# Sixteen-head attentions: the first sequence's key rows sent from SyncE's queue behind the queries' rows instead of from ScalarE's

## The chip, the cores and the metric

The kernel runs on one core of one Trainium2 chip. The metric is the device time of one execution in microseconds. A core has TensorE (PE; its weight loads are listed as PEld), VectorE (DVE), ScalarE (ACT), GpSimd (POOL) and SyncE (SP), each with its own stream of instructions, and 16 DMA engines. A DMA is issued by one of the engines' queues (here SyncE's, ScalarE's or GpSimd's), occupies that engine while it is issued, and adds to a semaphore when its data has landed.

## What is computed

Four decoder layers, each of three blocks (attn, xattn, ffn), on 8 sequences of 256 tokens with 128 features; every block is added to x. Three of the twelve blocks concern the change. All are attentions of sixteen heads with eight features a head:

```python
# L1_xattn: queries and keys from normalised x, values from the context, causal, then a two-layer GELU block
q = (kq @ Wq + bq); k = (kq @ Wk + bk); v = (ctx @ Wv + bv)        # each as [8, 16 heads, 256, 8]
out = softmax(q k^T + shifted causal mask) v
y = gelu(out @ W1 + b1) @ W2 + b2
# L2_xattn: queries from normalised x, keys and values from the context, a drawn mask, scale 128 ** -0.5
out = softmax(where(mask == 0, -1e20, q k^T) / sqrt(128)) v;  y = out @ Wo.T + bo
# L3_attn: latent attention of x, causal, scale 8 ** -0.5
```

## The kernel before

One function, `attention16` (line 983), does all three: x1 (L1_xattn, tiles named x_), x2 (L2_xattn, tiles named x_ too) and a3 (L3_attn, tiles named a_). The eight sequences are eight units; the sixteen heads of a unit are taken in eight pairs. Scores have to be near to float32, but the matmuls run in bf16: so queries and keys are each split in three bf16 pieces (GpSimd, `split_in_three`, L1130 to L1133), and the six products of pieces that matter (`PRODUCTS`) are stacked along the contraction. A stack has eight rows for each of the eight features of a head: six rows of pieces, one row for the maxima and one of zeros. The rows are laid into `queries` and `keys` by DMA from `pieces`, one DMA for each of the six rows on each side.

SyncE does that, in `stack(u)` for unit u: it waits until the queries' pieces are made (`split`), sends one row of zeros (L1088) and six rows of queries, waits for the keys' pieces and sends six rows of keys (L1092). These thirteen DMAs count on `stacked[u % 2]`. Unit 0 is an exception in the kernel before: SyncE leaves its keys out (`continue`), and ScalarE sends them in `stack_first_keys` (L1484), after its copy of unit 0's values. `set_constant_rows(ring)` (L1071, L1073) sends three rows that don't depend on data, once for each of four rings: for ring 0 at the very start, for rings 1 to 3 behind unit 0's stack. In x2 SyncE also loads the mask twice for each unit (L1079). `store_rows(u)` (L1097) sends the maxima's pieces into the queries.

The work runs by slots, one slot for each pair, each engine with the same list of slots. Ahead of the scores, unit u is normalised (VectorE L1158), turned (TensorE L1275, copied by ScalarE to `xnT`, L1447), projected to queries (L1281, ScalarE L1453), keys (L1285, L1453) and values (L1292, L1462). Units 0 and 1 go through this before the first scores. TensorE's order at the start is thus: tokens, queries, keys, values of unit 0; the same of unit 1; the scores of pairs 0 to 7 (L1310, masks L1330 or L1334), with unit 2's projections between; the scores of pair 8, the first of unit 1; the turning of unit 0's maxima (L1355). The scores of pair 0 wait for `stacked[0]`, those of pair 8 for `stacked[1]`:

```python
                if p == 0:
                    pe.wait_ge(stacked[u % 2], (u // 2 + 1) * STACK_DMAS * 16)
```

VectorE takes the maxima of each pair (L1170, L1171, L1173) and after eight pairs splits them in pieces (L1184 to L1188); the shifted scores, TensorE's L1322 from slot 12 on, wait for the stored rows of maxima, and ScalarE's exponentials (L1469) for them. GpSimd may make the next unit's pieces only when the last unit's thirteen DMAs have landed:

```python
                if u >= 1:
                    pool.wait_ge(stacked[(u - 1) % 2], ((u - 1) // 2 + 1) * STACK_DMAS * 16)
```

Of the kernel before, what the change touches and what calls it, by code (L numbers as in the profile page):

```python
# [982 lines left out]
def attention16(nc, g, w, name, tag, scale, from_x, causal, values_from_x=False, tail=None):  # L983
# [3 lines left out]
    PRODUCTS = ((0, 0), (1, 0), (2, 0), (0, 1), (1, 1), (0, 2))  # L987
    STEP = 8
# [14 lines left out]
    with ExitStack() as ctx:  # L1003
# [5 lines left out]
        pieces = sb("pieces", [P, 2, PIECES, T], BF16)  # L1009
        queries, keys = (sb(n, [P, RINGS, PAIRS, T], BF16) for n in ("queries", "keys"))  # L1010
# [10 lines left out]
        else:  # L1021
# [9 lines left out]
        xn_ready, xT_made, q_made, k_made, v_made, split = (  # L1031
            sem(n) for n in ("xn_ready", "xT_made", "q_made", "k_made", "v_made", "split"))
        tokens_taken, q_taken, k_taken, v_taken, maxima_taken, mix_taken, y_taken = (
            sem(n) for n in ("tokens_taken", "q_taken", "k_taken", "v_taken", "maxima_taken", "mix_taken", "y_taken"))
        stacked, rows_stored = ([sem(f"{n}{b}") for b in range(2)] for n in ("stacked", "rows_stored"))
# [11 lines left out]
        norm_in, tokens_in, q_in, k_in, v_in = (lambda slot, early=e: unit_at(slot + early) for e in (13, 12, 11, 10, 9))  # L1047
# [20 lines left out]
        @block.sync  # L1068
        def _(sp):
            def set_constant_rows(ring):  # L1070
                sp.dma_start(keys[MAX_ROW::STEP, ring, :, :], max_keys[:, :]).then_inc(constant_rows[ring], 16)  # L1071
                for dst in (queries, keys):
                    sp.dma_start(dst[MAX_ROW + 1::STEP, ring, :, :], zeros[:, :]).then_inc(constant_rows[ring], 16)  # L1073

            def load_masks(u):
                if u >= 2:
                    sp.wait_ge(mask_ready, u - 1)
                for i, which in enumerate((g.mask_qk, g.mask_kq)):
                    sp.dma_start(mask_int[:, u % 2, i, :, :], which[u * HALVES:(u + 1) * HALVES, :, :].rearrange("n p k -> p n k"))\  # L1079
                      .then_inc(mask_loaded[u % 2], 16)  # L1080

            def stack(u):
                for which, dst in enumerate((queries, keys)):
                    sp.wait_ge(split, 2 * u + which + 1)
                    if which == 0:
                        if u >= RINGS:
                            sp.wait_ge(shifted, (u - RINGS + 1) * PAIRS)
                        sp.dma_start(queries[MAX_ROW::STEP, u % RINGS, :, :], zeros[:, :]).then_inc(stacked[u % 2], 16)  # L1088
                    if which == 1 and u == 0:
                        continue  # L1090
                    for slot, of in enumerate(PRODUCTS):
                        sp.dma_start(dst[slot::STEP, u % RINGS, :, :], pieces[:, which, of[which], :]).then_inc(stacked[u % 2], 16)  # L1092

            def store_rows(u):
                sp.wait_ge(max_split, u + 1)
                for k in range(PIECES):
                    sp.dma_start(queries[MAX_ROW + STEP * k::STACK, u % RINGS, :, :], max_pieces[:, u % 2, k, :])\  # L1097
                      .then_inc(rows_stored[u % 2], 16)

            sp.wait_ge(max_keys_ready, 2)  # L1100
            set_constant_rows(0)
            for slot in slots:
                if norm_in(slot) is not None and not causal:
                    load_masks(norm_in(slot))
                if maxima_in(slot) is not None:
                    store_rows(maxima_in(slot))
                if v_in(slot - 1) is not None:
                    stack(v_in(slot - 1))
                if v_in(slot - 1) == 0:
                    for ring in range(1, RINGS):  # L1110
                        set_constant_rows(ring)
# [327 lines left out]
        @block.scalar  # L1439
        def _(a):  # L1440
            a.wait_ge(g.loaded[name], 16)

            def take_tokens(u):
                a.wait_ge(xT_made, u + 1)
                if u >= 1:
                    a.wait_ge(v_made, u)
                a.activation(xnT[:, :], ps_p[:, 0:T], ACT.Copy).then_inc(tokens_taken, 1)  # L1447

            def take_projection(which, u):
                a.wait_ge((q_made, k_made)[which], u + 1)  # L1450
                if u >= 1:
                    a.wait_ge(split, 2 * u)
                a.activation(rest[:, which, :], ps_p[:, 0:T], ACT.Identity, bias=w[("q_bias", "k_bias")[which]])\  # L1453
                    .then_inc((q_taken, k_taken)[which], 1)

            def take_values(u):
                a.wait_ge(v_made, u + 1)
                if u == 0:
                    a.wait_ge(ones_ready, 1)
                if u >= KEPT:  # L1460
                    a.wait_ge(weighed, (u - KEPT + 1) * GROUPS)
                a.activation(v_ones[:, u % KEPT, :, :, 0:HD].rearrange("p j h d -> p (j h) d"),  # L1462
                             ps_p[:, 0:T].rearrange("p (n d) -> p n d", d=HD), ACT.Copy).then_inc(v_taken, 1)

            def take_probs(r):
                a.wait_ge(shifted, r + 1)
                if r >= HELD:
                    a.wait_ge(weighed, (r - HELD) // 2 + 1)
                a.activation(probs[:, r % HELD, :, :], ps_z[:, :, 0:WIDE], ACT.Exp, scale=scale).then_inc(exped, 1)  # L1469

            def take_sums(n):
                a.wait_ge(weighed, n + 1)
                if n >= 2:
                    a.wait_ge(back_made, n - 1)
                a.activation(sumsT[:, n % 2, :], ps_o[:, 0:T], ACT.Copy).then_inc(sums_ready, 1)

            def take_mixed(u):
                a.wait_ge(mixT_made, u + 1)
                a.activation(mixT[:, u, :], ps_p[:, 0:T], ACT.Copy).then_inc(mix_taken, 1)

            def stack_first_keys():
                a.wait_ge(split, 2)
                for slot, of in enumerate(PRODUCTS):
                    a.dma_start(keys[slot::STEP, 0, :, :], pieces[:, 1, of[1], :]).then_inc(stacked[0], 16)  # L1484

            for slot in slots:
                r = slot - BEHIND
                if sums_in(r) is not None:
                    take_sums(sums_in(r))
                if pair_at(r) is not None:  # L1490
                    take_probs(r)
                if tail and mix_in(r) is not None:
                    take_mixed(mix_in(r))
                if tokens_in(slot) is not None:
                    take_tokens(tokens_in(slot))
                if q_in(slot) is not None:
                    take_projection(0, q_in(slot))
                if k_in(slot) is not None:
                    take_projection(1, k_in(slot))
                if v_in(slot) is not None:  # L1500
                    take_values(v_in(slot))
                if v_in(slot) == 0:
                    stack_first_keys()
            if tail == "mlp":
                for t in range(TURNS):
                    for c in range(4):
                        a.wait_ge(up_made, t * 4 + c + 1)
                        if t >= 2:
                            a.wait_ge(mlp_made, t - 1)
                        a.activation(hT[:, t % 2, c, :], ps_s[:, c // 2, c % 2, :], ACT.Gelu, bias=w["b1"][:, c:c + 1])\  # L1510
                            .then_inc(gelu_ready, 1)
# [2159 lines left out]
```

## Time and profile before

| what | value |
|---|---|
| median of 3 runs | 2074.45 us (2067.26 to 2081.59) |
| profiled execution, span | 2099.1 us (the page gives no time around the span) |
| TensorE matmul busy | 1629.8 us (78%) |
| VectorE busy | 1224.3 us (58%) |
| ScalarE busy | 846.3 us (40%) |
| GpSimd busy | 456.8 us (22%) |
| mean granted TensorE clock | 0.840 |
| x1 begins | at about 364 us |
| x2 begins | at about 997 us |
| a3 begins (after its weights are combined) | at about 1398 us |

Issuing a DMA isn't counted as busy; it stands in an engine's timeline as SPq or ACTq. A row of the timeline gives start, duration (of a merged group from the first start to the last end), engine, line, operation, output and inputs, the number of instructions, and in brackets the idle time before it with what ended it.

### The profile page before, as it was taken

What the parts mean: (1) busy time and instruction counts of PE and PEld (TensorE: products, weight loads), DVE (VectorE), ACT (ScalarE), POOL (GpSimd) and SP (SyncE); (2) the same over time, 40 slices, a digit from 0 to 9 for tenths busy, and PEclk for the clock granted to TensorE, in tenths of its full rate; (3) what the DMA queues carried; (4) which work ended last, traced back from release to release, by engine and by line L of the source; (5) the groups of instructions that cost most, each with busy time, mean ns of one, the idle gap of its engine ahead of it and who ended that gap; (6) DMA issues with size and microseconds to landing.
All of it is one profiled execution on the core that took longest, in us unless ns stands there. A gap on an engine that the chain in (4) does not pass through costs nothing. (4 is left out here: it accounts for less than half of the span.)

```text
span 2099.1 us, 34839 instructions
## 1 busy us (share of the span) xinstructions
PE 1629.8 (78%) x12344; PEld 1130.1 (54%) x12368; DVE 1224.3 (58%) x4316; ACT 846.3 (40%) x1790; POOL 456.8 (22%) x611
## 2 busy tenths in 40 slices
PE   3359556798957887757699889968867777999888
PEld 2138343455525776755254456744535654677666
DVE  5965745476176898844566333337747776666322
ACT  1133326255323776753255434324543310333322
POOL 0002000320013334320532000012202114655111
PEclk8665777699978898978799989978987866999979
DMA  2000000321015567640522000012210000000000
GB/s 82 0 11 1 9 29 19 89 52 36 1 66 190 196 211 254 216 165 7 153 66 61 2 17 0 0 56 59 57 67 1 0 0 1 3 2 2 3 0 21
DMA packets 79748, 115.69 MB, mean 55 GB/s; under 512 B 8416, under 2 KB 60512, under 8 KB 78816
## 3 DMA queue, kind: packets, MB, share of 16 engines
q0 software_dynamic: 18432, 67.38, 9.3%
q1 hardware_dynamic: 58560, 45.00, 7.7%
q8 instruction: 96, 1.57, 0.3%
q10 hardware_dynamic: 2592, 1.18, 0.2%
q14 instruction: 68, 0.56, 0.1%
HBM read 88.95 MB, written 1.05 MB: 43 GB/s over the span
## 5 line engine op out<-in xcount | busy, mean ns | idle before, releaser
L2398 POOL DMA_INDIRECT f_rows<-tree_table,f_index x128 | 125.8, 983 | 312.9 <-DVE f_index L2458 153.5
L1469 ACT ACTIVATE x_probs<-x_ps_z 128x768 f32<-128x768 f32 (+1 forms) x128 | 117.4, 917 | 101.9 <-PE x_ps_z L1334 66.0
L2615 PE MATMUL f_ps_o<-f_rows,shared_sb 128*128 128x128 f32 x1024 | 127.8, 287 | 33.6 <-ACT f_rows L2687 33.6
L2687 ACT ACTIVATE f_rows<-f_rows,f_low_act 128x128 f32<-128x128 f32 x512 | 153.0, 387 | 0.8
L2615 PEld LDWEIGHTS f_ps_o<-f_rows,shared_sb 128*128 128x128 f32 x1024 | 123.2, 201 | 39.0 <-ACT f_rows L2687 34.9
L2497 DVE CUSTOM_DVE_ANT_0 f_rows<-f_rows,f_xn 128x128 f32<-128x128 f32 x512 | 112.6, 287 | 20.7 <-DMA f_rows<-tree_table,f_index 13.2
L1173 DVE TENSOR_REDUCE x_minus_max<-x_ps_s 128x4 f32<-128x1024 f32 x64 | 78.1, 1224 | 61.8 <-PE x_ps_s L1334 61.5
L3133 ACT ACTIVATE r_probs<-r_ps_z 128x768 f32<-128x768 f32 x64 | 51.9, 811 | 67.8 <-PE r_ps_z L3024 67.8
L1867 PE MATMUL f_ps_h<-f_xnT,weights 128*128 128x512 f32 x144 | 76.2, 657 | 2.4 <-ACT f_hT L1932 2.4
L1879 PEld LDWEIGHTS f_ps_y<-weights,f_hT 128*128 128x128 f32 x576 | 69.8, 192 | 14.3 <-issue 12.6
L1932 ACT ACTIVATE f_hT<-f_ps_h,weights 128x512 f32<-128x512 f32 x72 | 48.6, 685 | 71.6 <-PE f_ps_h L1867 69.9
L1846 DVE SCALAR_TENSOR_TENSOR x_tokens<-f_ps_y,f_chosen,x_tokens 128x128 f32 (+1 forms) x128 | 36.0, 344 | 68.1 <-PE f_ps_y L1879 67.9
L1879 PE MATMUL f_ps_y<-weights,f_hT 128*128 128x128 f32 x576 | 73.3, 278 | 0.0
L1469 ACT ACTIVATE a_probs<-a_ps_z 128x768 f32<-128x768 f32 x64 | 51.9, 810 | 41.7 <-PE a_ps_z L1330 41.6
L1347 PE MATMUL x_ps_o<-x_probs,x_v_ones 128*32 128x256 f32 (+1 forms) x1024 | 64.9, 361 | 2.5 <-DVE x_mixed L1198 2.5
L2597 PE MATMUL f_ps_in<-shared_sb,f_act 128*128 128x128 f32 x192 | 34.5, 350 | 39.5 <-ACT f_maskedT L2674 26.0
L1322 PE MATMUL x_ps_z<-x_queries,x_keys 64*128 64x256 bf16 (+1 forms) x512 | 47.5, 264 | 20.7 <-ACT x_probs L1469 18.0
L3015 PE MATMUL r_ps_z<-r_queries,r_keys 64*128 64x256 f32 (+1 forms) x512 | 59.1, 349 | 2.6 <-ACT r_probs L3133 2.5
L2605 PE MATMUL f_ps_d<-weights,f_maskedT 128*128 128x128 f32 (+2 forms) x384 | 56.9, 302 | 5.0 <-ACT f_maskedT L2674 5.0
L2889 DVE TENSOR_REDUCE r_minus_max<-r_ps_s 128x2 f32<-128x256 f32 x64 | 27.2, 425 | 56.9 <-PE r_ps_s L3024 56.9
L1170 DVE TENSOR_REDUCE x_minus_max<-x_ps_s 128x2 f32<-128x256 f32 x64 | 27.0, 422 | 54.0 <-PE x_ps_s L1330 53.7
L2833 POOL TENSOR_TENSOR r_q_swapped<-r_q_swapped,weights 128x256 f32<-128x256 f32 x64 | 46.5, 726 | 54.2 <-DVE r_q_swapped L2881 53.9
(652 smaller groups left out, 4145.2 us busy)
## 6 DMA issues: line engine op xcount, KB each, us to landing
x_queries<-x_pieces SPq DMA_DIRECT2D x96, 64.0 KB, 2.1
x_keys<-x_pieces SPq DMA_DIRECT2D x84, 64.0 KB, 2.1
a_queries<-a_pieces SPq DMA_DIRECT2D x48, 64.0 KB, 2.1
weights<-w_L_ffn SPq DMA_DIRECT2D x1, 2985.5 KB, 10.2
a_keys<-a_pieces SPq DMA_DIRECT2D x42, 64.0 KB, 2.1
weights<-w_L_ffn SPq DMA_DIRECT2D x1, 2449.0 KB, 10.5
weights<-w_L_ffn SPq DMA_DIRECT2D x1, 2176.0 KB, 8.3
f_rows<-tree_table,f_index POOLq DMA_INDIRECT x128
```

The source lines that it names most:

```text
L1173: last = v.tensor_reduce(peaks.rearrange("p j h -> p h j"), scores.rearrange("p h (j k) -> p h j k", j=HALVES), AX.X, ALU.max, negate=True)
L1347: last = pe.matmul(out[V1 * i:V1 * (i + 1), a:T], v_ones[:, u % KEPT, half, SIDE * group + i, :], probs[:, r % HELD, i % 2, at:at + T - a] ...
L1469: a.activation(probs[:, r % HELD, :, :], ps_z[:, :, 0:WIDE], ACT.Exp, scale=scale).then_inc(exped, 1)
L1867: pe.matmul(ps_h[:, i % 2, :], w["up"][:, i * P:(i + 1) * P], xnT[:, :], start=True, stop=True).then_inc(up_made, 1)
L1879: last = pe.matmul(out, hT[:, i % 4, j * P:(j + 1) * P], w["down"][:, i * P:(i + 1) * P], start=c == 0, stop=c == CH - 1 and e < E)
L2398: pool.indirect_dma_start(rows[:, place(u, j), tree, :], None, g.tree_table, bass.IndirectOffsetOnAxis(index[:, u % 2, low, j * TREES + tr ...
L2497: last = v.tensor_tensor_reduce(row, row, xn[:, u % KEPT, j, :], 1.0, 0.0, ALU.mult, ALU.add, low_act[:, u % 3, j * TREES + tree, f:f + 1])
L2605: last = pe.matmul(ps_d[:, j, :], maskedT[0:k, i, :], w["out"][0:k, i * P:(i + 1) * P], start=i == 0, stop=i == ALL - 1)
L2615: last = pe.matmul(ps_o[:, low, j, :], g.ident, rows[:, place(u, j), tree, OUT + f * D:OUT + (f + 1) * D], start=k == 0, stop=k == TREES * ...
L2687: last = a.activation(row, row, ACT.Copy, scale=low_act[:, u % 3, j * TREES + tree, f:f + 1])
L3015: pe.matmul(ps_z[:, i, out], keys[rows, u % RINGS, k:k + P], queries[rows, u % RINGS, p, q:T], start=q == 0, stop=False)
L3133: a.activation(probs[:, r % HELD, :, :], ps_z[:, :, 0:WIDE], ACT.Exp).then_inc(exped, 1)
```

## The change

SyncE no longer leaves out unit 0's keys, so `stack(0)` sends all thirteen DMAs, and ScalarE's `stack_first_keys` is gone. The count on `stacked[0]` stays thirteen.

```diff
@@ stack(u), SyncE
-                    if which == 1 and u == 0:
-                        continue
                     for slot, of in enumerate(PRODUCTS):
                         sp.dma_start(dst[slot::STEP, u % RINGS, :, :], pieces[:, which, of[which], :]).then_inc(stacked[u % 2], 16)
@@ ScalarE
-            def stack_first_keys():
-                a.wait_ge(split, 2)
-                for slot, of in enumerate(PRODUCTS):
-                    a.dma_start(keys[slot::STEP, 0, :, :], pieces[:, 1, of[1], :]).then_inc(stacked[0], 16)
-
@@ ScalarE's slots
                 if v_in(slot) is not None:
                     take_values(v_in(slot))
-                if v_in(slot) == 0:
-                    stack_first_keys()
```

ScalarE at the start of x1, before (x_xnT is the copy of the turned tokens, x_rest of queries and keys, x_v_ones of the values; the first three rows are unit 0, the last three unit 1):

```order
L1447 ACTIVATE x_xnT<-x_ps_p 128x256
L1453 ACTIVATE x_rest<-x_ps_p,weights 128x256 x2
L1462 ACTIVATE x_v_ones<-x_ps_p 128x32x8
L1484 DMA x_keys<-x_pieces 16x8x256 x6
L1447 ACTIVATE x_xnT<-x_ps_p 128x256
L1453 ACTIVATE x_rest<-x_ps_p,weights 128x256 x2
L1462 ACTIVATE x_v_ones<-x_ps_p 128x32x8
```

and in the changed kernel:

```order
L1445 ACTIVATE x_xnT<-x_ps_p 128x256
L1451 ACTIVATE x_rest<-x_ps_p,weights 128x256 x2
L1460 ACTIVATE x_v_ones<-x_ps_p 128x32x8
L1445 ACTIVATE x_xnT<-x_ps_p 128x256
L1451 ACTIVATE x_rest<-x_ps_p,weights 128x256 x2
L1460 ACTIVATE x_v_ones<-x_ps_p 128x32x8
```

The six DMAs between the values of unit 0 and the tokens of unit 1 are gone; nothing else moves on ScalarE.

SyncE at the start of x2, before (x_max_keys and x_zeros are the constant rows, of ring 1 and ring 3 here with ring 2 between; x_mask_int is unit 1's mask; the last three rows are unit 1's stack):

```order
L1088 DMA x_queries<-x_zeros 16x8x256
L1092 DMA x_queries<-x_pieces 16x8x256 x6
L1071 DMA x_keys<-x_max_keys 16x8x256
...
L1073 DMA x_keys<-x_zeros 16x8x256
L1079 DMA x_mask_int<-mask_qk 128x2x256
L1079 DMA x_mask_int<-mask_kq 128x2x256
L1088 DMA x_queries<-x_zeros 16x8x256
L1092 DMA x_queries<-x_pieces 16x8x256 x6
L1092 DMA x_keys<-x_pieces 16x8x256 x6
```

and in the changed kernel:

```order
L1088 DMA x_queries<-x_zeros 16x8x256
L1090 DMA x_queries<-x_pieces 16x8x256 x6
L1090 DMA x_keys<-x_pieces 16x8x256 x6
L1071 DMA x_keys<-x_max_keys 16x8x256
...
L1073 DMA x_keys<-x_zeros 16x8x256
L1079 DMA x_mask_int<-mask_qk 128x2x256
L1079 DMA x_mask_int<-mask_kq 128x2x256
L1088 DMA x_queries<-x_zeros 16x8x256
L1090 DMA x_queries<-x_pieces 16x8x256 x6
L1090 DMA x_keys<-x_pieces 16x8x256 x6
```

Six DMAs come in ahead of the nine constant rows, the masks and unit 1's stack. In x1 and a3 it is the same without the masks.

## Rows read from the trace of the kernel before

**Rows 1.** The page's first line.
```profile
span 2099.1 us, 34839 instructions
```

**Rows 2.** ScalarE's timeline at the start of x1 and x2 (start us, us, ...).
```profile
376.89 3.92 ACTq L1484 DMA_DIRECT2D x_keys<-x_pieces  x6
380.91 0.38 ACT L1447 ACTIVATE x_xnT<-x_ps_p 128x256 f32<-128x256 f32 x1 [4.59 <-issue]
...
1012.89 0.38 ACT L1447 ACTIVATE x_xnT<-x_ps_p 128x256 f32<-128x256 f32 x1 [6.05 <-issue]
```

**Rows 3.** TensorE's timeline: tokens of sequence 1, then score(0), in x1, x2, a3.
```profile
376.37 0.69 PE L1275 MATMUL x_ps_p<-shared_sb,x_xn 128*128 128x128 f32 x2 [0.47 <-ACT x_v_ones L1462]
...
387.88 0.50 PE L1310 MATMUL x_ps_s<-x_keys,x_queries 64*128 64x128 bf16 x4
...
1006.89 0.69 PE L1275 MATMUL x_ps_p<-shared_sb,x_xn 128*128 128x128 f32 x2 [0.47 <-ACT x_v_ones L1462]
...
1018.12 0.61 PE L1310 MATMUL x_ps_s<-x_keys,x_queries 64*128 64x256 bf16 x4
...
1406.48 0.69 PE L1275 MATMUL a_ps_p<-shared_sb,a_xn 128*128 128x128 f32 x2 [0.47 <-ACT a_v_ones L1462]
...
1417.91 0.50 PE L1310 MATMUL a_ps_s<-a_keys,a_queries 64*128 64x128 bf16 x4
```

**Rows 4.** TensorE's timeline: score(8) in x1, x2, a3.
```profile
399.75 0.34 PE L1310 MATMUL x_ps_s<-x_keys,x_queries 64*128 64x128 bf16 x4
...
1029.89 0.39 PE L1310 MATMUL x_ps_s<-x_keys,x_queries 64*128 64x256 bf16 x4
...
1427.73 0.34 PE L1310 MATMUL a_ps_s<-a_keys,a_queries 64*128 64x128 bf16 x4 [0.54 <-DMA a_keys<-a_pieces]
```

**Rows 5.** SyncE's queue: constants, sequence 1's rows, in x1, x2, a3.
```profile
379.18 0.60 SPq L1071 DMA_DIRECT2D x_keys<-x_max_keys  x1
...
384.35 0.60 SPq L1073 DMA_DIRECT2D x_keys<-x_zeros  x1
385.58 0.53 SPq L1088 DMA_DIRECT2D x_queries<-x_zeros  x1
...
390.01 3.80 SPq L1092 DMA_DIRECT2D x_keys<-x_pieces  x6
...
1011.12 0.64 SPq L1071 DMA_DIRECT2D x_keys<-x_max_keys  x1
...
1018.47 0.54 SPq L1088 DMA_DIRECT2D x_queries<-x_zeros  x1
...
1022.90 3.80 SPq L1092 DMA_DIRECT2D x_keys<-x_pieces  x6
...
1410.93 0.63 SPq L1071 DMA_DIRECT2D a_keys<-a_max_keys  x1
...
1417.36 0.53 SPq L1088 DMA_DIRECT2D a_queries<-a_zeros  x1
...
1422.41 3.80 SPq L1092 DMA_DIRECT2D a_keys<-a_pieces  x6
```

**Rows 6.** The page's DMA issues: count, KB each, median us to landing.
```profile
x_keys<-x_pieces SPq DMA_DIRECT2D x84, 64.0 KB, 2.1
```

**Rows 7.** GpSimd's timeline: x1's sets for queries and keys; x2's masks, sequence 1.
```profile
383.20 0.40 POOL L1130 CAST x_pieces<-x_rest 128x256 bf16<-128x256 f32 x1 [6.35 <-ACT x_rest L1453]
...
385.50 0.40 POOL L1130 CAST x_pieces<-x_rest 128x256 bf16<-128x256 f32 x1
...
1021.03 3.64 POOL L1139 TENSOR_SCALAR x_masks<-x_mask_int 128x1024 bf16<-128x1024 int32 x1 [1.19 <-DMA x_mask_int<-mask_kq]
```

**Rows 8.** The tile x_keys, 1026.0 to 1026.8 us: x2's last two key issues.
```profile
DMA to landing us min/median/max: 2.0/2.9/3.7
```

**Rows 9.** Busy time by stretch in a3 (stretch, length, engines' busy us, granted clock, DMA share, GB/s).
```profile
1423.00:1430.00 7.00, 5.75 (x61) 3.02 (x60) 5.87 (x13) 3.00 (x5) 1.97 (x4) 1.00 0.28 66
1432.50:1438.50 6.00, 4.94 (x43) 2.74 (x44) 3.41 (x9) 1.68 (x3) 0.03 (x1) 0.51 0.27 61
```

## The prediction

> **What bounds the kernel now.** The span is 2099.1 us [rows 1]. The kernel is a row of layers, each with its own schedule, and no engine bounds all of them, so busy shares say nothing on this change. Only three layers call `attention16`: x1 (L1_xattn), x2 (L2_xattn, masked) and a3 (L3_attn). In each, the change touches the first twenty microseconds or so, in which the pipeline fills. I read the engines' timelines there: first ScalarE, where the removed instructions stand, then TensorE, which waits for it, then SyncE's queue, where they go, and GpSimd, which makes the pieces. I call the eight sequences 0 to 7; score(n) is TensorE's score work on pair n, eight pairs to a sequence, so score(0) needs sequence 0's stacked rows and score(8) those of sequence 1.
>
> Three things are to be seen.
>
> First, ScalarE is the late engine in the fill. It issues its six DMAs from 376.89 for 3.92 us and only then copies sequence 1's transposed tokens, at 380.91 [rows 2]. TensorE had these ready at 376.37 + 0.69 = 377.06 [rows 3]. So the copy is 3.7 us late; in x2 it is at 1012.89 [rows 2] for tokens ready at 1006.89 + 0.69 = 1007.58 [rows 3], 5.2 us late (the wait for GpSimd's pieces stands ahead of the DMAs). In a3 tokens and score(0) lie 11.43 us apart against 11.23 in x2 [rows 3], so about 5.4 us. All of sequence 1's projections stand behind that copy, and score(0) stands behind these in TensorE's own order. None of the three score(0) rows shows idle time put down to a DMA [rows 3].
>
> Second, SyncE's queue is also nearly full. Behind the queries' rows of sequence 0 it issues nine constant rows, in x2 two masks, and then sequence 1's thirteen DMAs. In x2 it goes from 1011.12 to 1018.47 without a pause (eleven issues, 0.67 us each); in x1 the constants end at 384.35 + 0.60 = 384.95 and sequence 1 begins at 385.58, as soon as its pieces are made [rows 5].
>
> Third, sequence 1's rows arrive just when score(8) wants them: in a3 score(8) at 1427.73 waits 0.54 us for a DMA of key rows [rows 4], in x2 the last of them lands at the moment of score(8) (below), and in x1 there is room.
>
> **What the change takes away.** ScalarE loses six issues and the wait ahead of them in each layer. If nothing else were late, score(0) would come 3.7, 5.2 and 5.4 us earlier. What is late next is the key rows. On SyncE they start where the first constant row starts now: 379.18, 1011.12, 1410.93 [rows 5]. Six key issues take 3.80 us [rows 5], with the 0.04 us to the next one 3.84; the last starts 3.80 - 0.60 = 3.20 us in, and a DMA of this kind lands 2.1 us after its start [rows 6]. So the keys are there 5.3 us after the start:
> - x1: 384.5 against 387.88 for score(0) now: 3.4 us earlier
> - x2: 1016.4 against 1018.12: 1.7 earlier
> - a3: 1416.2 against 1417.91: 1.7 earlier
>
> TensorE would be ready at 384.1, 1012.9 and 1412.5, so in all three the key rows decide.
>
> **What the change adds.** Everything behind the keys on SyncE starts up to 3.84 us later: the nine constant rows, the masks, and sequence 1's rows. Sequence 1's pieces aren't the limit: GpSimd may overwrite the pieces only when all thirteen DMAs of sequence 0 have landed, and needs 385.50 - 383.20 = 2.30 us for a set [rows 7]. In x1 that is 384.5 + 2.3 = 386.8, while SyncE gets there later:
> - x1: the constants end at 379.18 + 3.84 + (384.95 - 379.18) = 388.79, so sequence 1 starts at 388.85 instead of 385.58. Its last key issue starts at 390.01 + 3.20 + 3.27 = 396.5 and lands at 398.6. score(8) is at 399.75 now [rows 4], and 3.4 us earlier TensorE would be ready at 396.4. It waits until 398.6: gain 1.15 us instead of 3.4.
> - x2: the queue has no pause to absorb anything, so the shift is 3.84. The last two key issues land after 2.9 us in the median and 3.7 at most [rows 8]; the last, behind which the next mask is sent, is the slow one: 1022.90 + 3.20 + 3.7 = 1029.8, which is score(8)'s 1029.89. With the change 1033.65: loss 3.75 us. The masks of sequence 1 are late too, but by 3.84 only: 1021.03 + 3.64 + 3.84 = 1028.5 [rows 7], before 1033.65.
> - a3: constants 1410.93 + 3.84 + 5.8, as in x1, so sequence 1 starts at 1420.6 instead of 1417.36, a shift of 3.25. Its last key lands at 1422.41 + 3.20 + 2.1 + 3.25 = 1430.95, against 1427.73: loss 3.2 us.
>
> Behind score(8) the maxima of sequence 0 are turned, split by VectorE, stored by SyncE, and the first shift waits for them; so what score(8) loses reaches the first probabilities and everything behind. The later rows keep their distance, as store and stack follow on the same queue. GpSimd's set for sequence 2 starts when sequence 1's rows have landed, later by as much, and has until SyncE comes to it after the maxima. I count all this at nothing.
>
> Not shown by any row of before is TensorE after such a wait: from its ready time (score(0) plus today's distance, 11.87, 11.77 and 9.82 us) score(8) now waits 398.6 - 396.4 = 2.2, 1033.65 - 1028.2 = 5.5 and 1430.95 - 1426.0 = 4.9 us. After the pause at 1430 to 1432.5 the granted clock was 0.51 for six microseconds, that is the 1.2 GHz level, against 1.00 before [rows 9]. Four score matmuls take 0.50 us at the lower level (score(0) in a3, rows 3) and 0.34 at the higher (score(8), rows 4). Lower bound: -0.5 us a layer, if the slow stretch is only moved forward and ends sooner; upper bound +1.5, if all TensorE work of a six-microsecond stretch takes half as long again with half of it on the path. I take 0.25 a layer, nearest to what one slow score costs, 0.8 in all.
>
> **Sum.** -1.15 + 3.75 + 3.2 + 0.8 = +6.6 us. The profiled execution has a span of 2099.1, which is 24.65 above the median of the runs, 2074.45 (2067.26 to 2081.59); the page gives no time around the span. The sum is a difference and is added to the median: 2081.1 us, 0.3% slower, and not to be told from no change. (1% is about what a measurement of this kernel can tell.)
>
> **A rule against the trace.** The issue of these DMAs is 0.60 us each, 3.84 for the six, against 2.1 us for one to land [rows 5, 6]. The Trainium skill (DMA: Bandwidth & Descriptors, section Issuing engines are not separate DMA queues) says that starting DMAs on several engines saves only the sequencer's issue time, usually small beside the DMA itself. The first half agrees with the trace; the second doesn't, since here six issues last nearly twice as long as a landing. By that rule the move would cost next to nothing and give the whole of ScalarE's time back. As a mechanism of this kernel: the key rows are no limit, and score(0) gains 3.7 + 5.2 + 5.4 = 14.3 us, 2060.2.
>
> **Rivals.**
> - A, faster: score(0) decides and sequence 1's rows are absorbed, because SyncE's issues run closer together or score(8) isn't what the fill hangs on. Gain 3.4 + 1.7 + 1.7 = 6.8, 2067.7. For it: the fill's late engine is ScalarE, by the plain rows. Against: a3's wait for key rows at score(8) [rows 4] is there already. 12%.
> - B, made good: the delay arises but is given back before each layer ends, since later waits for rows shrink or the clock is granted sooner; x1's gain stays. About -1, 2073.5. For it: each layer has seven more sequences and TensorE isn't always the bound. Against: SyncE's order carries the delay along. 15%.
> - C, slower by over 1%: the longer pause ahead of score(8) leaves TensorE at the 1.2 GHz level well into the steady part. At 0.50 against 0.34 us the price is half of the full-clock time; it takes 14 us of TensorE-bound work in each layer to make 7 us a layer, 21 + 5.85 = 27 in all, 2101. It decides if the low clock lasts some 20 us beyond the pause. Against: the clock recovers now within about six [rows 9]. 5%.
> - D, the rule above: no limit from the keys, 2060.2. 3%.
>
> The forecast has 65%.
>
> **Range.** From A's 2067.7 to the forecast with the clock's upper bound (3 x 1.5 in place of 0.8: 2084.8) stand the likely cases; the runs of before lie 7 us to each side of their median, and the median of a few new ones may move by most of that. 2066 to 2092 leaves out D, most of C and the tails. Slower by over 1% is above 2095.2: C, 5%. Faster by over 1% is below 2053.7, where no case stands; 2% for what I overlooked. The rest, 93%, is within 1%.
>
> **What would show it right or wrong.** In all three layers ScalarE's copy of sequence 1's tokens follows the end of TensorE's transposes within 0.2 us, and score(0) waits for a DMA of key rows and comes at about 3.4, 1.7 and 1.7 us less than now from the layer's first transposes. The nine constant rows start 3.84 us later. score(8) waits for a DMA of key rows in all three, 2, 5 and 5 us, and the distance from the first transposes to score(8) is 1.2 us shorter in x1 and 3.8 and 3.2 us longer in x2 and a3. Wrong I would be if score(8) came earlier in x2 or a3, or if it came late and the layer's end did not.

## The result, and the profile after

| | median us | ratio to before (95% interval) |
|---|---|---|
| before, 19 runs beside the changed kernel | 2072.97 (2065.12 to 2083.12) | |
| changed kernel, 19 runs | 2080.09 (2072.74 to 2085.98) | 1.0028 (1.0015 to 1.0041) |

The changed kernel is slower by 0.28%, 5.8 us by the ratio (3.1 to 8.5) and 7.1 by the medians; forecast was 6.6. That is far below 1%, yet the interval leaves out no change.

The profiled execution took 2078.33 us with a span of 2076.5. Its first lines against [rows 1]:

```profile
span 2076.5 us, 34863 instructions
PE 1637.3 (79%) x12368; PEld 1130.0 (54%) x12368; DVE 1221.7 (59%) x4316; ACT 845.8 (41%) x1790; POOL 461.4 (22%) x611
```

The profile of before had a span of 2099.1, so the two spans say the opposite of the runs. They are single executions (that of before lies over 15 us above the slowest of the 19 timed runs), and from the first transposes of x1 to those of x2 they differ by 31 us (632.3 against 601.4), nearly all of it in layers that this change does not touch (x1 itself ends 0.65 us apart). Hence everything below counts from each layer's own first transposes. In before these are

```profile
368.10 0.66 PE L1275 MATMUL x_ps_p<-shared_sb,x_xn 128*128 128x128 f32 x2 [6.80 <-DVE x_masks L1223]
...
1000.36 0.66 PE L1275 MATMUL x_ps_p<-shared_sb,x_xn 128*128 128x128 f32 x2 [6.27 <-DVE x_ident L1226]
...
1399.96 0.66 PE L1275 MATMUL a_ps_p<-shared_sb,a_xn 128*128 128x128 f32 x2 [3.17 <-DVE a_masks L1223]
```

TensorE's timeline of the changed kernel, in each layer the first transposes, score(0) and score(8) (the rows that answer to [rows 3, 4]), and in x1 sequence 1's tokens too:

```profile
369.17 0.66 PE L1273 MATMUL x_ps_p<-shared_sb,x_xn 128*128 128x128 f32 x2 [6.80 <-DVE x_masks L1221]
...
377.44 0.69 PE L1273 MATMUL x_ps_p<-shared_sb,x_xn 128*128 128x128 f32 x2 [0.47 <-ACT x_v_ones L1460]
...
385.39 0.50 PE L1308 MATMUL x_ps_s<-x_keys,x_queries 64*128 64x128 bf16 x4 [0.18 <-DMA x_keys<-x_pieces]
...
399.97 0.50 PE L1308 MATMUL x_ps_s<-x_keys,x_queries 64*128 64x128 bf16 x4 [2.33 <-DMA x_keys<-x_pieces]
...
970.61 0.66 PE L1273 MATMUL x_ps_p<-shared_sb,x_xn 128*128 128x128 f32 x2 [6.29 <-DVE x_ident L1224]
...
986.99 0.61 PE L1308 MATMUL x_ps_s<-x_keys,x_queries 64*128 64x256 bf16 x4 [3.84 <-DMA x_keys<-x_pieces]
...
1003.45 0.61 PE L1308 MATMUL x_ps_s<-x_keys,x_queries 64*128 64x256 bf16 x4 [4.95 <-DMA x_keys<-x_pieces]
...
1378.90 0.66 PE L1273 MATMUL a_ps_p<-shared_sb,a_xn 128*128 128x128 f32 x2 [3.17 <-DVE a_masks L1221]
...
1395.61 0.50 PE L1308 MATMUL a_ps_s<-a_keys,a_queries 64*128 64x128 bf16 x4 [4.17 <-DMA a_keys<-a_pieces]
...
1409.69 0.50 PE L1308 MATMUL a_ps_s<-a_keys,a_queries 64*128 64x128 bf16 x4 [2.81 <-DMA a_keys<-a_pieces]
```

All six score rows now carry a wait for a DMA of key rows; before, one did [rows 3, 4]. Distances from the first transposes, us (the end is the last turning back of sums, L1362 before and L1360 now; first shifted is the first score with its maximum taken off, L1322 before and L1320 now):

| | score(0) | score(8) | first shifted | end |
|---|---|---|---|---|
| x1 before, now | 19.8, 16.2 | 31.65, 30.8 | 37.9, 37.8 | 167.4, 166.7 |
| x2 before, now | 17.8, 16.4 | 29.5, 32.8 | 36.7, 40.8 | 201.3, 205.2 |
| a3 before, now | 17.95, 16.7 | 27.8, 30.8 | 34.5, 37.7 | 161.8, 164.7 |

The start is quicker up to score(0) in all three. At score(8) 0.85 us of x1's 3.6 are left, and x2 and a3 have lost 3.3 and 3.0. The first shifted scores come -0.1, +4.1 and +3.1 us later (unrounded, +7.2 in all), and the layers' ends -0.65, +3.95 and +2.95, in all +6.2. The runs' 5.8 (3.1 to 8.5) agrees.

On ScalarE the stall is gone (x1 shown): the copy of sequence 1's tokens waits 0.78 us for TensorE's transposes and for nothing else (compare [rows 2]):

```profile
377.00 0.38 ACT L1460 ACTIVATE x_v_ones<-x_ps_p 128x256 f32<-128x256 f32 x1 [3.05 <-PE x_ps_p L1292]
378.17 0.38 ACT L1445 ACTIVATE x_xnT<-x_ps_p 128x256 f32<-128x256 f32 x1 [0.78 <-PE x_ps_p L1273]
```

SyncE's queue in x1: the keys, the first and the last constant row, the start of sequence 1's stack and its keys (compare [rows 5]):

```profile
380.08 3.80 SPq L1090 DMA_DIRECT2D x_keys<-x_pieces  x6
383.93 0.60 SPq L1071 DMA_DIRECT2D x_keys<-x_max_keys  x1
...
389.06 0.60 SPq L1073 DMA_DIRECT2D x_keys<-x_zeros  x1
389.70 0.60 SPq L1088 DMA_DIRECT2D x_queries<-x_zeros  x1
390.34 4.28 SPq L1090 DMA_DIRECT2D x_queries<-x_pieces  x6
394.67 3.80 SPq L1090 DMA_DIRECT2D x_keys<-x_pieces  x6
```

The keys start at 380.08 and TensorE is released at 385.39, 5.31 us later. From the keys to sequence 1's stack there is no pause left; it starts 20.5 us after the first transposes, against 17.5 before. One of its six queries' issues took 1.08 us (the 4.28 above); why is told in the last section.

### The profile page after: what moved, and what is told of

It is laid out like the page before. It is cut to its first block and busy times, and to the rows that moved or that the text cites. A ratio compares the mean times of both kernels' runs of the same rounds, so it can differ in the third digit from the quotient of the medians.

```text
span 2076.5 us, 34863 instructions
## 1 busy us (share of the span) xinstructions
PE 1637.3 (79%) x12368; PEld 1130.0 (54%) x12368; DVE 1221.7 (59%) x4316; ACT 845.8 (41%) x1790; POOL 461.4 (22%) x611
## 3 DMA queue, kind: packets, MB, share of 16 engines
HBM read 88.95 MB, written 1.05 MB: 43 GB/s over the span
## 5 line engine op out<-in xcount | busy, mean ns | idle before, releaser
L1870 PEld LDWEIGHTS f_ps_y<-weights,f_hT 128*128 128x128 f32 x576 | 70.7, 194 | 14.3 <-issue 12.6
L1320 PE MATMUL x_ps_z<-x_queries,x_keys 64*128 64x256 bf16 (+1 forms) x512 | 47.7, 265 | 20.0 <-ACT x_probs L1467 17.7
L1308 PE MATMUL x_ps_s<-x_keys,x_queries 64*128 64x256 bf16 (+1 forms) x512 | 50.3, 278 | 16.6 <-DMA x_keys<-x_pieces 13.2
```

The costliest lines, as they stand in the source:

```text
L1308: pe.matmul(ps_s[:, r % 2, i, out], stack_of(queries, u, p, i, half * P, P), stack_of(keys, u, p, i, 0, out.stop - out.start), start=half ...
L1870: last = pe.matmul(out, hT[:, i % 4, j * P:(j + 1) * P], w["down"][:, i * P:(i + 1) * P], start=c == 0, stop=c == CH - 1 and e < E)
```

## Experiments

All are told by the same distances. In the runs, a ratio of 0.001 is 2.07 us. A difference between two changed kernels is that of their ratios to before, and its own interval is wider than either.

**The queue ahead of sequence 1, shortened.** The changed kernel, with the constant rows of two rings sent later:

```diff
                 if v_in(slot - 1) == 0:
-                    for ring in range(1, RINGS):
+                    set_constant_rows(1)
+                if v_in(slot - 1) == 1:
+                    for ring in range(2, RINGS):
                         set_constant_rows(ring)
```

> The changed kernel with six of the nine constant rows (rings 2 and 3) sent behind sequence 1's stack instead of ahead of it, in all three layers. Times are counted from a layer's first transposes to score(0) and score(8). Theory (the loss is the length of SyncE's queue ahead of sequence 1's thirteen DMAs): score(0) as in the changed kernel, 16.2, 16.4 and 16.7 us in x1, x2, a3; sequence 1's stack then waits for its pieces, 2.3 us behind the landing of sequence 0's keys, so score(8) at 28.5, 30.1 and 29.4 us (31.65, 29.5, 27.8 before; 30.8, 32.8, 30.8 in the changed kernel); in all about 1 us faster than before and 7 to 8 us faster than the changed kernel. Rival (the loss is in the start itself, the clock after the pauses or the pieces' wait): score(8) stays within 1 us of the changed kernel and the time too.

Measured: 2070.83 us, ratio 0.9991 (0.9975 to 1.0007), 1.9 us below before and 7.7 below the changed kernel by the ratios. score(0) 16.2, 16.4, 16.7; score(8) 28.9, 29.2, 28.9, within 0.9 us of the theory in each layer. The interval doesn't separate it from before, but it does from the changed kernel. Score(8) in the three layers:

```profile
399.14 0.34 PE L1310 MATMUL x_ps_s<-x_keys,x_queries 64*128 64x128 bf16 x4 [0.39 <-DMA x_keys<-x_pieces]
...
1007.88 0.39 PE L1310 MATMUL x_ps_s<-x_keys,x_queries 64*128 64x256 bf16 x4 [1.35 <-DMA x_keys<-x_pieces]
...
1410.23 0.34 PE L1310 MATMUL a_ps_s<-a_keys,a_queries 64*128 64x128 bf16 x4 [1.50 <-DMA a_keys<-a_pieces]
```

The waits of 2.3, 5.0 and 2.8 us are down to 0.4, 1.35 and 1.5, and the matmuls that follow take 0.34 and 0.39 us instead of 0.50 and 0.61. Nothing was done to sequence 0's part of the start, so what the changed kernel lost, it lost in the queue. In this profile the gain shrinks towards the ends of the layers (+0.7, +0.8, +1.6 against before, though the first shifted scores stood at -2.1, -0.2 and +1.1); the twelve runs show no such loss (this execution, 2079.43 us, was one of their slowest), and I take the ends of one execution as good to a microsecond or two a layer.

**SyncE's part alone.** The kernel before, ScalarE's DMAs and all, with six more on SyncE, rows of zeros into a spare tile (its allocation and a wait for them behind the last slot are left out here):

```diff
                 if v_in(slot - 1) == 0:
+                    for row in range(6):
+                        sp.dma_start(spare[row::STEP, :, :], zeros[:, :]).then_inc(spare_sent, 16)
                     for ring in range(1, RINGS):
```

> The kernel before, ScalarE still sending the keys, with six more DMAs of rows of zeros into a spare tile on SyncE, behind the queries' rows of sequence 0, in all three layers: SyncE's part of the change alone. Theory: score(0) unchanged at 19.8, 17.8 and 18.0 us from the first transposes; score(8) unchanged in x1 (31.7; its rows would land at 30.5), 3.75 us later in x2 (33.3) and 3.2 later in a3 (31.0); time 7 to 8 us above before. Rival (SyncE's extra issues are absorbed, and the changed kernel's loss came from ScalarE's queue being gone or from the clock): score(8) within 1 us of before in all three and no change of time.

Measured: 2082.45 us, ratio 1.0041 (1.0025 to 1.0057), +8.5 us. score(0) 19.8, 17.7, 17.95; score(8) 31.7, 32.6, 31.5 (31.7, 33.3 and 31.0 were expected); first shifted scores +0.4, +3.9, +3.7. The rival falls: ScalarE's queue is as before, the stall too, and the loss is there.

**The cost doubled.** The same six DMAs in the changed kernel.

> The changed kernel with the same six DMAs into a spare tile behind sequence 0's keys: the suspected cost doubled. Theory: score(0) as in the changed kernel; score(8) 3.84 us later in all three layers, x1 now too (34.6, 36.7, 34.6 us from the first transposes), 11.5 us above the changed kernel and 18 above before, plus up to 1 for the clock. Rival (a threshold that the change has already passed, so that more issues are hidden by the same wait): well under 6 us above the changed kernel.

Measured: 2091.49 us, ratio 1.0084 (1.0067 to 1.0100), 17.4 us above before, 11.6 above the changed kernel by the ratios. score(8) 34.7, 36.45, 34.7: 3.9, 3.6 and 3.9 us behind the changed kernel. x1 pays in full now, as its room is used up:

```profile
386.81 0.50 PE L1312 MATMUL x_ps_s<-x_keys,x_queries 64*128 64x128 bf16 x4 [0.18 <-DMA x_keys<-x_pieces]
...
405.34 0.50 PE L1312 MATMUL x_ps_s<-x_keys,x_queries 64*128 64x128 bf16 x4 [6.25 <-DMA x_keys<-x_pieces]
```

**The pieces' wait taken away.** The changed kernel with two buffers for the bf16 pieces:

```diff
-        pieces = sb("pieces", [P, 2, PIECES, T], BF16)
+        pieces = sb("pieces", [P, 2, 2, PIECES, T], BF16)
...
-                if u >= 1:
-                    pool.wait_ge(stacked[(u - 1) % 2], ((u - 1) // 2 + 1) * STACK_DMAS * 16)
+                if u >= 2:
+                    pool.wait_ge(stacked[u % 2], (u // 2) * STACK_DMAS * 16)
```

> The changed kernel with two buffers for the bf16 pieces, so that GpSimd needn't wait for sequence 0's rows before it makes sequence 1's pieces. Theory (SyncE's issues are the limit, not the pieces): sequence 1's stack starts where it does in the changed kernel, score(8) at 30.8, 32.8 and 30.8 us from the first transposes within 0.3, and no change of time against the changed kernel. Rival (the pieces, held back until the late keys land, are what makes sequence 1's rows late): score(8) comes 1 us or more earlier in each layer, the time 3 us or more below the changed kernel.

Measured: 2074.58 us, ratio 1.0002 (0.9987 to 1.0018), 5.4 us below the changed kernel. This went half against me. At score(8), 31.25, 32.0 and 31.4, x1 and a3 are no earlier (0.45 and 0.6 us later, more than the 0.3 allowed), though GpSimd made sequence 1's pieces 5.0 and 7.2 us sooner; SyncE's issues are the limit there. x2 came 0.9 us earlier, just under the rival's 1 us. But the time moved by as much as the rival said, and no change had been expected. Most of the gain isn't at the place that the rival named: in x1 it is in the later sequences, whose end came at 163.3 instead of 166.7. x2's end is 2.3 us earlier, of which 1.6 is there at the first shifted scores already, and a3's is where it was. The same edit on the kernel before:

> The kernel before with two buffers for the pieces and nothing else. In the changed kernel this gave 5 to 6 us, though score(8) hardly moved in x1 and a3; there the later sequences of x1 got 3.4 us shorter. Theory (GpSimd's wait for the last sequence's rows costs in the later sequences whatever the start looks like): score(8) within 0.5 us of before in all three layers, x1's end 3 to 4 us earlier, 4 us in all. Rival (it only mends what the change had spoiled): no change against before.

Measured: 2069.67 us, ratio 0.9983 (0.9969 to 0.9998), 3.5 us below before. score(0) and score(8) stayed (19.8, 17.7, 18.0 and 31.7, 29.7, 27.75), the ends came at 163.3, 201.6 and 158.3, so -4.1, +0.3 and -3.5. It is a gain of its own, not a mending of the change, though the ends of this one execution add up to twice what the runs show. What the traces show beside it: VectorE's split of the maxima runs longer while GpSimd makes pieces. In a3 before, then with two buffers:

```profile
L1187 DVE CAST a_max_pieces<-a_max_rest x8: 280/280/486, 1430.2 to 1543.4; 16x256 bf16<-16x256 f32 x8
L1188 DVE TENSOR_TENSOR a_max_pieces<-a_max_rest,a_max_pieces x8: 411/846/851, 1430.7 to 1543.8; 16x256 bf16<-16x256 f32 x8
```

```profile
L1187 DVE CAST a_max_pieces<-a_max_rest x8: 280/280/282, 1399.0 to 1508.8; 16x256 bf16<-16x256 f32 x8
L1188 DVE TENSOR_TENSOR a_max_pieces<-a_max_rest,a_max_pieces x8: 412/414/414, 1399.3 to 1509.1; 16x256 bf16<-16x256 f32 x8
```

(count, then shortest, median and longest in ns). Before, six of the eight took 837 to 851 ns and two 411 and 414, and one CAST took 486: 2.8 us in all above the short durations, of a3's 3.5. In x1 the same two lines have 2.1 us to give, of its 4.1. And the changed kernel has long ones too in a3 (six, 553 to 845 ns), with two buffers none, yet its a3 ended no sooner. So the long instructions are neither enough nor always on the path, and how the two buffers save their time stays open.

**The stall removed without a longer queue.** From the kernel before, ScalarE sends the keys two at a time behind its copies for sequence 1:

```diff
-                if v_in(slot) == 0:
-                    stack_first_keys()
...
                     take_tokens(tokens_in(slot))
+                if tokens_in(slot) == 1:
+                    stack_first_keys((0, 1))
...
                     take_projection(0, q_in(slot))
+                if q_in(slot) == 1:
+                    stack_first_keys((2, 3))
...
                     take_projection(1, k_in(slot))
+                if k_in(slot) == 1:
+                    stack_first_keys((4, 5))
```

> The kernel before, with ScalarE still sending sequence 0's keys, but two at a time between its copies for sequence 1 (two behind the tokens, two behind the queries, two behind the keys) instead of all six ahead of them: the stall goes and SyncE's queue stays as before. Theory: score(0) at 16.2, 15.0 and 15.1 us from the first transposes in x1, x2, a3 (19.8, 17.8, 18.0 before); sequence 1's stack starts as before, so score(8) at 28.2, 29.5 and 27.8 us (31.65, 29.5, 27.8 before): a gain in x1 alone, 3 us in all against before. Rival (ScalarE's stall is what costs in all three layers): gains of 3.5, 2.7 and 2.8 us at score(8), 9 us in all.

Measured: 2068.24 us, ratio 0.9985 (0.9968 to 1.0002), -3.1 us. score(0) 16.0, 14.7, 16.1 and score(8) 28.2, 28.6, 28.3. The ratio's interval just reaches no change; the places in the traces decide between the two. Score(0) comes 3.8, 3.0 and 1.9 us sooner, and at score(8) 3.4 us are left in x1, 0.9 in x2 and -0.5 in a3: the theory's 3, 0 and 0, not the rival's 9. x2's 0.9 went again in the next microseconds (first shifted scores at 36.6 against 36.7). a3 is where the theory was a little off: its pieces for sequence 1 waited for the late keys and were begun 1.1 us later than before (0.5 in x1). score(8) in x1 and in a3:

```profile
395.81 0.34 PE L1310 MATMUL x_ps_s<-x_keys,x_queries 64*128 64x128 bf16 x4 [1.54 <-DMA x_keys<-x_pieces]
...
1401.70 0.34 PE L1310 MATMUL a_ps_s<-a_keys,a_queries 64*128 64x128 bf16 x4 [0.76 <-DMA a_keys<-a_pieces]
```

**Versions that beat both.** Two rings' constants late and two buffers, on the changed kernel; then these two with ScalarE sending the keys between its copies, on the kernel before.

> The changed kernel with the constant rows of rings 2 and 3 behind sequence 1's stack and with two buffers for the pieces. Theory: sequence 1's stack then waits for neither; score(0) 16.2, 16.4, 16.7; score(8) as soon as TensorE is ready or a little later, 28.1, 29.2 and 26.7 us from the first transposes; 4 us from the start and 3 to 4 from x1's later sequences: 2065 us. Rival (the two gains are the same one): 2070, as with the constant rows alone.

> From the kernel before: ScalarE sends sequence 0's keys two at a time between its copies, the constant rows of rings 2 and 3 go behind sequence 1's stack, and the pieces have two buffers. Theory: score(0) at 16.2, 15.0, 15.1 us and score(8) at 28.1, 27.1, 24.9 us from the first transposes, 8.5 us from the start and 3 to 4 from x1's later sequences, about 12 us below before, 2061. Rival (TensorE at the lower clock or VectorE takes over the start): score(8) as forecast, but the first shifted scores less than half as much earlier, and no better than 2067.

Measured: 2062.79 us, ratio 0.9946 (0.9925 to 0.9967), and 2061.87 us, ratio 0.9937 (0.9916 to 0.9957): 11 and 13 us below before. score(8) at 27.0, 28.9, 27.5 and at 26.6, 26.5, 27.0. Both rivals fall; the gains of the queue and of the buffers add up (17 us below the changed kernel, 7.7 and 5.4 by themselves). In the last kernel score(8) waits for no DMA any more in any layer:

```profile
395.37 0.34 PE L1312 MATMUL x_ps_s<-x_keys,x_queries 64*128 64x128 bf16 x4
...
996.42 0.39 PE L1312 MATMUL x_ps_s<-x_keys,x_queries 64*128 64x256 bf16 x4
...
1393.82 0.34 PE L1312 MATMUL a_ps_s<-a_keys,a_queries 64*128 64x128 bf16 x4
```

a3 didn't follow the forecast of 24.9: score(0) came at 16.85 instead of 15.1, after 3.2 us of waiting for key rows. x1 was better than forecast, 27.0 and 26.6 instead of 28.1. Between the two versions the intervals overlap, so ScalarE's part in the last one isn't shown to be worth anything.

## Why the prediction was right

**The step at score(0)**: forecast 3.4, 1.7 and 1.7 us earlier, measured 3.6, 1.4 and 1.2. The key rows take the place of ScalarE's stall as the late arrival, as said. TensorE was ready 16.0, 12.55 and 12.55 us from the first transposes, which is where the forecast had it. (By the forecast's own rows the copies were 3.85 and 5.31 us late, not 3.7 and 5.2; the sum doesn't use this.) x2 and a3 gained less because the six key issues took 4.17 and 4.26 us instead of 3.80: in x2 there was a pause of 0.38 us between two of them, whose cause no row shows, in a3 one took 1.05. x1 gained more because the queries' six took 3.81 us with ScalarE's DMAs gone, 3.97 beside them.

**The step at score(8)**: forecast -1.15, +3.75 and +3.2, measured -0.85, +3.3 and +3.0. Adding six DMAs to SyncE alone gives it (before_plus6), doubling them doubles it (after_plus6), and sending six others later takes it away (ring23_late). What is left of the differences, 0.3, 0.45 and 0.2 us, is where one slow issue fell, told next and in the last section: in x1 it moved into sequence 1's queries (1.08 us, unforeseen), in a3 out of them (1.22 us before, which the forecast had carried along) and into sequence 0's keys (1.05 us).

**The landing of the last key row in x2** was right in the sum for a wrong reason. The forecast gave it 3.7 us because the next mask is sent behind it. The mask is sent behind it in the changed kernel too, and there it lands in 2.1:

```profile
DMA to landing us min/median/max: 2.1/2.1/2.1
```

(the tile x_keys, 1001.2 to 1001.6 us, the last two key issues). What made up for it is a slow issue ahead: the six queries took 5.08 us instead of 3.81. The term was mis-sized by 1.6 us one way and 1.3 the other, and that the two nearly cancel was not foreseen.

```profile
992.44 0.54 SPq L1088 DMA_DIRECT2D x_queries<-x_zeros  x1
993.02 5.08 SPq L1090 DMA_DIRECT2D x_queries<-x_pieces  x6
998.15 3.80 SPq L1090 DMA_DIRECT2D x_keys<-x_pieces  x6
```

In the traces these are one event. In either kernel one issue 25 to 27 us from the first transposes is slow, and it and the one or two DMAs just ahead of it land late, in 3.3 to 3.7 us. Before, it is the second mask's, and the last key stands two ahead of it; now it is one of the queries':

```profile
1027.38 1.66 SPq L1079 DMA_DIRECT2D x_mask_int<-mask_kq  x1
...
995.60 1.86 SPq L1090 DMA_DIRECT2D x_queries<-x_pieces  x1
```

**The masks in x2** were made 3.65 us later and were done 4.9 us before score(8), so they held nobody, as costed.

**The clock's term**: forecast +0.25 us a layer. The granted clock did fall at score(8), in all three layers (columns as in [rows 9]; ahead of and behind the wait in x1, x2 and a3, with the stretches at the lower level in full):

```profile
395.20:397.60 2.40, 2.32 (x17) 1.45 (x16) 1.10 (x3) 0.47 (x1) 0.00 (x0) 1.00 0.46 109
398.60:412.30 13.70, 9.77 (x80) 5.17 (x82) 8.19 (x18) 3.02 (x5) 4.39 (x8) 0.50 0.20 49
992.90:998.40 5.50, 5.00 (x34) 2.44 (x34) 5.38 (x7) 1.33 (x3) 3.47 (x1) 1.00 0.57 164
1002.80:1013.00 10.20, 8.70 (x38) 2.20 (x39) 7.33 (x10) 0.00 (x0) 7.96 (x9) 0.50 0.26 75
1403.00:1406.80 3.80, 3.72 (x24) 1.68 (x22) 2.19 (x5) 0.95 (x2) 0.00 (x0) 0.67 0.44 104
1409.00:1422.60 13.60, 10.46 (x86) 5.69 (x88) 8.18 (x18) 2.48 (x4) 4.39 (x8) 0.50 0.19 45
```

Before, the same layers have their low stretch a few microseconds later, behind the pause ahead of the first shifted scores, and it is about half as long or less:

```profile
404.20:411.10 6.90, 5.51 (x46) 2.83 (x42) 4.06 (x9) 2.04 (x4) 0.00 (x0) 0.51 0.33 79
1035.70:1039.10 3.40, 2.97 (x13) 0.89 (x14) 2.30 (x4) 0.00 (x0) 2.65 (x1) 0.50 0.28 66
1431.70:1438.50 6.80, 4.94 (x43) 2.74 (x44) 4.21 (x11) 1.68 (x3) 0.75 (x2) 0.50 0.23 54
```

From score(8) to the first shifted scores the changed kernel needs 0.8, 0.8 and 0.1 us more than before, which is 1.7 in all; by the ends of the layers 0.8 of it is left. That is the size forecast, though the single ends are no sharper than that and no run takes the clock's part by itself. The forecast thought of a slow stretch of six microseconds or of one that is only moved forward. It lasts 10 to 14 us instead, and little of it lies on the path. In a3 the wait was 2.8 us and not the 4.9 forecast, since TensorE was still partly at the lower level (0.67) during the scores ahead and reached score(8) later.

**The total.** The forecast called its difference not to be told from no change. With 19 runs on each side it can be told.

**The rivals.** A (absorbed): x2 and a3 refute it, as does before_plus6. B (made good later): the ends keep +6.2 of the +7.2. C (the clock stays low): the low stretch doubled to 13.7 us at most, short of the some 20 that it needed, and the time stayed far below 1%. D, by the Trainium skill (DMA: Bandwidth & Descriptors, section Issuing engines are not separate DMA queues), that the issue time saved by a second engine is usually small beside the DMA itself: measured, six issues are worth 3.6 to 3.9 us a layer at score(8) once there is no room (after_plus6) against 2.1 us for a landing. So the rule's second half doesn't hold for these DMAs of 64 KB.

## What to carry to other kernels

A DMA queue is a resource with a length: before moving DMAs from a stalled engine to SyncE, list what stands behind them there until the next deadline, and how much pause is in between; the stall that goes is worth only what the queue's next customer can wait. Look first for what in that queue can move behind the deadline (here constant rows of rings that are needed a sequence or two later), since this gave 7.7 us here where the choice of the engine took 5.8. And read a gain at the place where it should arise and again one deadline later.

## What was not expected of the hardware

Now and then an issue on SyncE's queue takes 1.0 to 2.2 us instead of 0.6, and the one or two DMAs just ahead of it can land in 3.5 us instead of 2.1. In the ten traces, from x1 to a3, 188 of 4365 issues took over 1.0 us, and all 188 overlap a packet of 16 KB of the DMA queue that the profile lists as `instruction`; of 254 such packets that overlap an issue, 188 come with a slow one. Here it is beside the slow issue in x2 (packets, MB, share of the 16 engines' time), before (1027 to 1028.6 us) and now (995.5 to 997):

```profile
q8 instruction: 1, 0.02, 5.9%
```

```profile
q8 instruction: 1, 0.02, 6.1%
```

The packets come at the same place of the program: in a3 at 17.9 us from the first transposes in before, before_plus6 and before_pieces2, and at 12.6 in the changed kernel and its four descendants. That is when TensorE gets to score(0) (18.0 us, and ready at 12.5), so they may be TensorE's own instructions on their way; this is argued, no row names their engine. An edit thus moves them too, and one that falls ahead of a deadline is worth its whole excess, 0.45 to 1.3 us here.

VectorE's instruction of 16x256 elements (L1188) takes 411 to 415 ns alone and 546 to 851 ns with GpSimd's piece-making beside it. Over the ten traces all 77 that overlap piece-making are long and the other 163 are short, 16 of them beside GpSimd's mask-making alone. L1185, of the same size but with one input in `ps_p` (PSUM), stays at 411 to 413 ns all 240 times, beside piece-making too. The Trainium skill (SBUF — State Buffer, section SBUF: two separate sides) says that VectorE and GpSimd meet at one shared port, held by one of them for a whole instruction. L1188 beside piece-making agrees with that. What sets it off from L1185 in these traces is that both its inputs are tiles in SBUF; nothing was varied by itself, and why the mask-making did no harm stays open.
